# A two-convolution kernel on one core: the first image's high halves on GpSimd from the fourteenth chunk on, and its sums on ScalarE

## The reference, cut to what matters

```python
x = x + conv3x3_per_image(gn(x), weights_of_image)   # layer 0
x = x + circular_conv3x3(gn(x), w1)                  # layer 1 (the reference goes through FFTs)
```

## Time and profile before

| | |
|---|---|
| median of 3 runs | 1730.44 us |
| the profiled execution | 1728.56 us |
| its span, first to last instruction | 1726.8 us |
| mean granted TensorE clock | 0.990 of full |
| PE (TensorE matmul) busy | 1630.3 us, 94% |
| PEld (TensorE weight load) busy | 1260.8 us, 73% |
| DVE (VectorE) busy | 1294.9 us, 75% |
| ACT (ScalarE) busy | 1144.3 us, 66% |
| POOL (GpSimd) busy | 112.0 us, 6% |

### The profile page before, as it was taken

One profiled execution on the slowest core, in us unless ns is written; L12 is line 12 of the kernel. 1 busy time (PEld: TensorE's weight loads), 2 busy tenths in 40 slices (PEclk: granted clock), 3 DMA queues, 4 the chain that ended last, 5 costly groups with the idle time before them and its releaser, 6 DMA issues.

```text
span 1726.8 us, 63815 instructions
## 1 busy us (share of the span) xinstructions
PE 1630.3 (94%) x28906; PEld 1260.8 (73%) x28906; DVE 1294.9 (75%) x1744; ACT 1144.3 (66%) x1029; POOL 112.0 (6%) x347
## 2 busy tenths in 40 slices
PE   5888888789899999999999999999999999999999
PEld 4787778655467777887688778867786778677766
DVE  5999899889977777777777777777777777777600
ACT  6888878589666666666666666666666666666444
POOL 0000000031100020002000200020002000100100
PEclk9999999989999999999999999999999999999999
DMA  9999999935466566666666666666666665665255
GB/s 386 421 421 422 422 422 421 379 92 161 119 199 211 201 198 211 210 201 198 213 207 201 198 212 208 200 199 211 210 200 198 209 212 185 213 206 204 112 203 203
DMA packets 99668, 409.99 MB, mean 237 GB/s; under 512 B 16883, under 2 KB 17384, under 8 KB 83048
## 3 DMA queue, kind: packets, MB, share of 16 engines
q1 hardware_dynamic: 98025, 405.94, 65.7%
q0 software_dynamic: 672, 0.08, 0.1%
q10 hardware_dynamic: 735, 0.37, 0.1%
HBM read 271.83 MB, written 134.50 MB: 235 GB/s over the span
## 4 chain that ended last, share of the span: by engine, by line
PE 75%; DVE 12%; issue 7%; ACT 4%; DMA 2%; DVEq 0%; ACTq 0%; SPq 0%; POOL 0%; POOLq 0%
PE ps L527 72%; DVE x L810 9%; ACT x L633 2%; DMA x<-x_pix 1%; ACT x L668 1%; ACT x L670 1%; DMA x<-wf 1%; DVE x L1013 1%; DVE x L864 1%; DVE stats L1030 1%; PE ps L452 1%; PE ps L453 0%; ACT x L674 0%; PE ps L456 0%; PE ps L463 0%
## 5 line engine op out<-in xcount | busy, mean ns | idle before, releaser
L527 PE MATMUL ps<-x,wc 64*64 64x512 f16 x24540 | 1339.9, 377 | 10.3 <-DVE x L1013 9.4
L527 PEld LDWEIGHTS ps<-x,wc 64*64 64x64 f16 x24540 | 992.7, 107 | 351.5 <-issue 21.4
L864 DVE SCALAR_TENSOR_TENSOR x<-xin,gnp,x 128x1028 f16<-128x1028 f32 x247 | 320.3, 1298 | 234.6 <-ACT x L633 234.5
L633 ACT ACTIVATE x<-xin,gnp 128x1028 f16<-128x1028 f32 x247 | 286.4, 1160 | 307.6 <-PE ps L527 302.4
L684 ACT ACTIVATE outb<-ps,bias 128x1024 f32<-128x1024 f32 x256 | 285.3, 1114 | 155.0 <-PE ps L527 155.0
L1013 DVE SCALAR_TENSOR_TENSOR x<-ps,gnp,x 128x1024 f16<-128x1024 f32 x256 | 325.1, 1270 | 24.3 <-ACT x L670 24.0
L452 PE MATMUL ps<-x 128*128 128x129 f16 x2048 | 254.1, 224 | 59.0 <-DVE x L810 58.6
L810 DVE SCALAR_TENSOR_TENSOR x<-x 128x2048 bf16<-128x2048 f32 x128 | 282.8, 2283 | 19.3 <-DMA x<-wf 17.4
L1030 DVE BATCH_NORM_STATS2 stats<-ps 128x6 f32<-128x512 f32 x440 | 283.6, 687 | 11.1 <-ACT x L674 8.5
L619 ACT ACTIVATE x<-x 128x2048 f16<-128x2048 f32 x128 | 240.1, 1908 | 52.6 <-PE ps L453 36.0
L452 PEld LDWEIGHTS ps<-x 128*128 128x128 f16 x2048 | 197.7, 98 | 78.6 <-DVE x L810 78.6
(11 more groups left out here) (144 smaller groups left out, 292.2 us busy)
## 6 DMA issues: line engine op xcount, KB each, us to landing
x<-x_pix SPq DMA_DIRECT2D x128, 1024.0 KB, 11.5
out<-outb SPq DMA_DIRECT2D x256, 512.0 KB, 3.7
xin<-x_tiles SPq DMA_DIRECT2D x239, 514.0 KB, 3.6
xin<-x_tiles SPq DMA_DIRECT2D x8, 642.5 KB, 4.1
x<-x_tiles SPq DMA_DIRECT2D x9, 514.0 KB, 7.2
w<-taps_scratch SPq DMA_DIRECT2D x60, 8.0 KB, 2.7
w<-taps_scratch SPq DMA_DIRECT2D x30, 16.0 KB, 3.1
taps_scratch<-x POOLq DMA_DIRECT2D x21, 3.0 KB, 1.8
```

Of the source, the lines that this page charges most:

```text
L527: return nc.tensor.matmul(to.rearrange("p (r w) -> p r w", w=NCOL), lhs, two, start=first, stop=last)
L633: nc.scalar.activation(planes[:, 0, a:a + w], x_at(g), ACT.Identity, scale=gnp[:, 1, b:b + 1]).then_inc(hi0_ready, 1)
L864: V.scalar_tensor_tensor(planes[:, 1, a:a + w], x_at(g), gnp[:, 1, b:b + 1], planes[:, 0, a:a + w], ALU.mult, ALU.subtract).then_inc(lo0_r ...
```

## The change

In image 0, the high halves of chunks 13 to 31 (`by_pool`) move from ScalarE to a TENSOR_SCALAR on GpSimd (`first_hi0`), each behind its chunk's pad and behind the wait for the job that frees its place. The high halves of chunks 0 to 12, and of image 1 on, stay on ScalarE. ScalarE takes the sums of all chunks of image 0 but the last three. The 21 taps DMAs move from GpSimd to SP, three at each of its steps 1 to 7. GpSimd does the wrap columns of chunk 7 after chunk 16's high half, those of chunk 15 after chunk 24's, and those of chunk 23 after its loop. VectorE waits on GpSimd's counter where GpSimd made the high half.

```diff
--- before.py
+++ after.py
@@ -64,7 +64,7 @@
 def by_act(b, n):
 
     if b == 0:
-        return n < TAIL0 and n % 4 != 3
+        return n < TAIL0
     return n < 2 if b == 1 else 0 < n < 3
 
 
@@ -147,6 +147,21 @@
     if g + HI_FIRST < LAP + NX:
         return g + HI_FIRST
     return ahead(g) if g + NSEVEN >= LAP + NX else None
+
+
+def by_pool(g):
+
+    return HI_FIRST <= g < NCH
+
+
+def hi0_count(g):
+
+    return g + 1 if g < HI_FIRST else g + 1 - (NCH - HI_FIRST)
+
+
+def spot_before(g):
+
+    return g - (LAP if g < LAP + NSEVEN else NSEVEN if g < TURN + NX else NX)
 
 
 def l1_chunk(h):
@@ -253,6 +268,7 @@
         pad_done = sem("pad_done")
         pool_pad = sem("pool_pad")
         hi0_ready = sem("hi0_ready")
+        pool_hi0 = sem("pool_hi0")
         lo0_ready = sem("lo0_ready")
         w0_ready = sem("w0_ready")
         lower_done = sem("lower_done")
@@ -418,6 +434,8 @@
                     load_x(g + NSEVEN + NX)
                 if TURN + NX <= g + 2 * NX < ALL:
                     load_x(g + 2 * NX)
+                if 0 < g < B:
+                    taps_out(sp, g, taps_rest)
                 if 8 <= n < 12 and b < B - 1:
 
                     if n == 8:
@@ -623,12 +641,12 @@
 
                 b, n = divmod(g, NCH)
                 w = loads(n)
-                if g < NCH:
+                if g < HI_FIRST:
                     act.wait_ge(pool_pad, g + 1)
                 else:
                     act.wait_ge(pad_done, g + 1 - NCH)
                 if g >= LAP:
-                    act.wait_ge(pe_done, JOB0[g - (LAP if g < LAP + NSEVEN else NSEVEN if g < TURN + NX else NX)] + 1)
+                    act.wait_ge(pe_done, JOB0[spot_before(g)] + 1)
                 a = nat_at(g)
                 nc.scalar.activation(planes[:, 0, a:a + w], x_at(g), ACT.Identity,
                                      scale=gnp[:, 1, b:b + 1]).then_inc(hi0_ready, 1)
@@ -694,7 +712,7 @@
                 early = g < ALL and g >= NCH and by_act(*divmod(g, NCH))
                 if early:
                     hi1(g)
-                if ahead_hi(g) is not None:
+                if ahead_hi(g) is not None and not by_pool(ahead_hi(g)):
                     hi0(ahead_hi(g))
                 if g < ALL and not early:
                     hi1(g)
@@ -733,10 +751,19 @@
                 if row_pad(g) is not None:
                     row, parts = row_pad(g)
                     link(ins)
-                    link(G.tensor_copy(row, gnp[parts, 0, 0:1].to_broadcast([32, XPITCH])))
+                    ins = G.tensor_copy(row, gnp[parts, 0, 0:1].to_broadcast([32, XPITCH]))
+                if by_pool(g) or row_pad(g) is not None:
+                    link(ins)
                     pool.sem_inc(pool_pad, 1)
                 else:
                     ins.then_inc(pool_pad, 1)
+
+            def first_hi0(g):
+
+                a = nat_at(g)
+                w = loads(g)
+                pool.wait_ge(pe_done, JOB0[spot_before(g)] + 1)
+                G.tensor_scalar(planes[:, 0, a:a + w], x_at(g), gnp[:, 1, 0:1], None, ALU.mult).then_inc(pool_hi0, 1)
 
             def ends(b, n):
 
@@ -747,23 +774,18 @@
             link(G.tensor_tensor(padm[:, :, :], gnp[:, 0, :].unsqueeze(2).to_broadcast([P, B, 2]),
                                  c("pmask").unsqueeze(1).to_broadcast([P, B, 2]), ALU.mult))
             G.tensor_tensor(gnp[:, 6, :], gnp[:, 0, :], gnp[:, 1, :], ALU.mult).then_inc(shift_x, 1)
-            for g in range(LAP + NX):
+            for g in range(NCH):
                 first_pad(g)
-            pool.wait_ge(zve, Z_TAPS)
-            pool.wait_ge(zdma, 16 * 4)
-            for b in range(1, B):
-                taps_out(pool, b, taps_rest)
-            for turn in range(NCH):
-                if LAP + NX <= turn + 9 < NCH:
-                    first_pad(turn + 9)
-                if turn - 1 in ENDS:
-                    ends(0, turn - 1)
+                if by_pool(g):
+                    first_hi0(g)
+                if g - NSEVEN - 2 in ENDS:
+                    ends(0, g - NSEVEN - 2)
             def products(out, a, z):
 
                 link(G.tensor_tensor(out, a, z, ALU.mult))
 
             for b in range(B):
-                for n in ENDS if b else ENDS[-1:]:
+                for n in ENDS if b else ENDS[2:]:
                     last = ends(b, n)
                 last.then_inc(wrapped, 1)
                 pool.wait_ge(seeded, b + 1)
@@ -860,7 +882,10 @@
 
                 b, n = divmod(g, NCH)
                 w, a = loads(n), nat_at(g)
-                ve.wait_ge(hi0_ready, g + 1)
+                if by_pool(g):
+                    ve.wait_ge(pool_hi0, g - HI_FIRST + 1)
+                else:
+                    ve.wait_ge(hi0_ready, hi0_count(g))
                 V.scalar_tensor_tensor(planes[:, 1, a:a + w], x_at(g), gnp[:, 1, b:b + 1],
                                        planes[:, 0, a:a + w], ALU.mult, ALU.subtract).then_inc(lo0_ready, 1)
```

## The result

The changed kernel is slower: 1740.69 us median (1740.3 to 1740.96) against 1729.86 (1728.99 to 1730.54), a ratio of 1.0063 with a 95% interval of 1.005 to 1.0076. That is 10.8 us more, where 5.2 us less had been forecast; it lies 1.7 us above the top of the range. The profiled execution took 1740.85 us, 12.3 more than the profiled one of before. Of experiment 8's kernel one execution in ten took 4400 us; it is left out there.

What follows compares the result with a forecast made beforehand. ScalarE was taken to bound image 0, VectorE close behind. The last pair was put at 448.3 + 5.2 + 2.0 = 455.5 against 460.72, so -5.2 us and 1725.2 us, range from just under 1720.0 to 1739.

Steps and rivals of the forecast that it cites:

- What bounds the kernel, and which point decides: Image 0: ScalarE slowest at 2.93 us a chunk, VectorE 2.70, TensorE 2.60; the last statistics pair at 460.72 decides.
- The low clock behind it: After image 0's last pair: TensorE's idle and the low clock behind it stay, priced at nothing, 1 us either way.
- ScalarE and VectorE: Image 0: ScalarE falls to 2.18 us a chunk, 2.0 charged for backlog; VectorE's chain to the pair from 68.5 to 58.5.
- lo1(9): VectorE instruction starting the counted chain to image 0's last pair: from 392.26 to 389.8 us, 2.5 earlier.
- the charge for held instructions: VectorE's lo0 held by GpSimd's halves: 0.34 us excess on the 15 halves of chunks 17 to 31, 5.2 us.
- GpSimd's 19 high halves: Chunks 13 to 31 of image 0: each half taken as 1.10 us on GpSimd, no row showing the operation there.
- the lower end: Low estimate for a 1028-column GpSimd half: 0.98 us, from a pad of 8 columns and a copy of 257.
- excess over one lo1: GpSimd's time per chunk, 1.54 us, beyond one lo1 of 1.20: 0.34 us lost by VectorE on each of 15 halves.
- the third rival: GpSimd's half becomes VectorE's clock at lo0: above about 1.4 us the gain is gone; at 1.9, 1739.4 us; chance 0.26.
- No blocking of VectorE: Rival: GpSimd does not hold lo0, the 5.2 us vanish, 10.4 us gained, 1720.0 us; chance 0.10.
- The second: Rival: GpSimd's half takes 1.3 to 1.6 us; 1.6 us earlier at 1.3, 3.4 later (1733.8) at 1.57; chance 0.20.
- Taps and queues: 21 taps DMAs moved to SP: nothing, at most 1 us; GpSimd's new waits for TensorE: nothing.

Runs made afterwards that it cites:

- experiment 8: Changed kernel with GpSimd's multiplication replaced by the f32-to-f16 conversion done twice, one waiting for the other: 1729.96 us against 1729.54 before, ratio 1.0004.
- experiment 7: Kernel before with seven extra GpSimd instructions at its start, to measure their lengths alone: 1731.32 us against 1729.94, one execution each.
- Experiment 3: Changed kernel with GpSimd's multiplication replaced by a plain f32-to-f16 copy, scale left out: 1722.85 us, ratio 0.9959 to the kernel before.
- Experiment 1: Kernel before with ScalarE taking the sums of all image 0 chunks below 29, every high half still on ScalarE: 1732.12 us against 1729.69, ratio 1.0013.
- Experiments 6: Changed kernel with the scale given to GpSimd's TENSOR_SCALAR as the constant 16 instead of a pointer: 1740.21 us, one execution.
- experiment 9: Changed kernel with GpSimd's multiplication replaced by a memset of the same high half, which reads nothing: 1722.38 us, one execution.
- experiment 5: Kernel before with only the 21 taps DMAs issued by SP instead of GpSimd: 1729.96 us against 1729.54, ratio 1.0.
- experiment 4: Changed kernel with only the odd chunks of 13 to 31 on GpSimd, the even ones on ScalarE: 1729.66 us, ratio 0.9999 to the kernel before.

## Why the prediction was wrong

**What bounds the kernel, and which point decides.** Right. Image 0 is where the time moved, the last pair moved it, and TensorE's idle behind it stayed at 4.4 us. The low clock behind it was priced at nothing with 1 us either way; in the profiled executions it made 1.5, which a kernel with an unchanged image 0 shows as well (experiment 7).

**ScalarE and VectorE.** Right where the forecast's length held. Experiment 3 had the pair at 455.82 for a forecast of 455.5, and VectorE's waits for ScalarE before lo1 shrank as described, from 3.1 us to 1.3 with those before the statistics. Its lo1(9) starts 30.7 us after TensorE's first job, for a forecast of 30.6, and the pair 65.0 us later, for 65.7. That the plain comparison comes out to 0.3 is partly luck: TensorE's first job came 0.9 us late in that execution, which hid that the charge for held instructions was about 1 us too high. Two of the sums are a tenth high (0.34 x 15 is 5.1, not 5.2; 387.5 + 2.18 is 389.7, not 389.8), which changes nothing. Experiment 1 shows what the rest rests on: the sums can move only if the halves leave ScalarE.

**GpSimd's 19 high halves: the step that failed.** I took 1.10 us, "the lower end plus the 0.07 by which the one-column pointer form exceeds the pad". It measured 2.90 where nothing held it. The lower end was the slope of a copy between 8 and 257 columns, and for a copy it was right (1.04 against 0.98). The instruction to come was not a copy. No row of before had a wide TENSOR_SCALAR, and a one-column one tells only the fixed part, 0.27 us; of the 2.54 ns for each further column it holds nothing. The upper end for it, 1.57, was again the copy's, and 5.7 was set aside for its stride. Experiments 6 and 7 exclude the pointer and the f16 output. The prediction's own sign of being wrong, a solitary half of over 1.5 us, is what came.

**What VectorE loses: the form was wrong too.** The forecast added 15 times "excess over one lo1" to VectorE's own work. At 2.90 + 0.44 - 1.20 = 2.14 that would be 32 us, and the pair near 483. What formed is the ring: a half and the lo0 that uses it in series, 4.09 us a chunk, with lo1 in GpSimd's shadow. From hi0(17) at 387.51, fifteen periods are 61.4 us and end at 448.9; the last lo0 started at 449.25. The sum agrees, not each period: three were 3.29 us, with GpSimd not held, and two were 5.67 and 5.50, with wrap columns or a row's pad between the halves. Experiment 8's 3.33 fits the form as well, 2.16 + 1.19 = 3.35. The ring becomes the pace where GpSimd's length + 1.2 passes TensorE's 2.6, near 1.4 us. That is not yet a loss against the kernel before, as the third rival had it: experiment 8, at 2.16, came out even.

**No blocking of VectorE.** This rival falls: lo0 was lengthened in experiment 3 and in the changed kernel (2.12 us at 376.18). The Trainium skill's page SBUF — State Buffer (Who interferes with whom) is right that a GpSimd instruction that reads SBUF and a VectorE one with two SBUF inputs collide and that one without a read does not; experiment 9 agrees, with all eighteen narrower memsets at 0.95 or 0.96 us beside lo0. That the second is blocked until the first's whole instruction ends the traces show for GpSimd behind lo0, but not for lo0 behind GpSimd (last section).

**The second and third rivals.** The third, GpSimd's half as the clock at lo0, with 0.26, names what happened, but its price does not hold: it was made for 1.9 us (1739.4), where experiment 8 took 1730 with 2.16, and at the real 2.9 the same rule gives the 32 us above. That the time came out only 1.3 us over its 1739.4 is luck. The estimate of 1.54 us by the GPSIMD Engine Reference of the Trainium skill (Elementwise — side-by-side cycle accounting) was nearer than mine but short by nearly half: 2.80 us for 1024 columns is 2.73 ns a column, 3.3 cycles at the page's 1.2 GHz. Its 2.6 cycles for a two-input TENSOR_TENSOR, an estimate of 2.2 us, compares with 1.89 measured.

**Taps and queues.** Right (experiment 5). That GpSimd's new waits and long instructions have pads behind them that others need was priced at nothing; in the changed kernel it is small beside the ring (the periods of 5.67 and 5.50), and in experiment 4 pads came 5.1 us late for ScalarE and one copy 3.2 us late on VectorE, where a gain had been expected.

**The range** went to 1739 because the case of longer halves was left out. An operation with no wide row on its engine should have kept its far end in the range.

## What to carry to other kernels

Price an instruction on an engine by a row of the same instruction there, of a similar width; a narrow one gives the fixed part alone and a copy gives the copy's slope. If there is none, the far end stays in the range, or the operation is reshaped into one that has a row: here the scale went into the weights, the multiplication became a conversion, and a loss of 10.8 us became a gain of 7.4. Where one engine feeds another chunk by chunk, compare its length, with what comes between and what holds it, with the pace of the rest. Where two engines also hold each other over a shared path, add their lengths round the loop first.

## What the runs showed of the hardware that was not expected

- GpSimd's TENSOR_SCALAR is 2.7 times as long as its copy of the same 1024 columns (2.80 and 1.04 us), and longer than a TENSOR_TENSOR multiplication (1.89), with f16 or f32 output; a constant instead of the pointer takes off 0.07 us.
- GpSimd behind lo0 waits for lo0's end (0.81 us in the ring, 1.09 where both began within 0.02 us at 394.1). lo0 behind GpSimd's 2.90 us waits only until about 0.93 us after that instruction's start. In the changed kernel, with GpSimd first and VectorE second:

```profile
369.50 2.90 POOL L766 TENSOR_SCALAR x<-xin,gnp 128x1028 f16<-128x1028 f32 x1 [0.21 <-POOL xin L750]
...
376.09 2.91 POOL L766 TENSOR_SCALAR x<-xin,gnp 128x1028 f16<-128x1028 f32 x1 [0.21 <-POOL xin L750]
...
390.80 2.91 POOL L766 TENSOR_SCALAR x<-xin,gnp 128x1028 f16<-128x1028 f32 x1 [0.20 <-POOL xin L750]
```

```profile
370.49 1.28 DVE L889 SCALAR_TENSOR_TENSOR x<-x,gnp 128x1028 f16<-128x1028 f32 x1
...
376.18 2.12 DVE L889 SCALAR_TENSOR_TENSOR x<-xin,gnp,x 128x1028 f16<-128x1028 f32 x1
...
391.44 1.56 DVE L889 SCALAR_TENSOR_TENSOR x<-xin,gnp,x 128x1028 f16<-128x1028 f32 x1
```

The lo0 at 376.18 ended 0.84 us late, so it got under way at 377.02, 0.93 after GpSimd's start; the one at 391.44 ended 0.28 late, under way at 391.72, 0.92 after. The one at 370.49, 0.99 after GpSimd's start, was not held at all, with 1.9 us of that instruction still to run. Behind experiment 3's conversion of 1.04 us lo0 got under way 0.84 or 0.85 us after the start (423.73 and 417.94), so almost as long after it as behind the instruction of 2.90. It looks as if only the first 0.9 us of either took the input; that is argued from these places.
- A small VectorE copy (3.47 us instead of 0.28, experiment 4) did wait for GpSimd's end, and the same copy waited for a GpSimd memset, which only writes (0.90 us instead of 0.28, experiment 9). The weights' L1079 (1.21 us instead of 0.35 at 407.50) was released 0.91 us after GpSimd got under way, like lo0. Which VectorE instructions are held for the read alone and which for the whole stays open.
- The low clock behind the same 4.4 us of TensorE idle lasted 5.0 us before the change and 8.2 after it. With image 0 as before it was 6.0 us in experiment 5 and 8.3 in experiment 7, so it differs without the change. Why stays open.
